# One transpose moved ahead of another, small VectorE operands placed in PSUM, one more pair of h scaled on VectorE, and new queue orders on four engines

## What is computed

```python
# conv: a decaying, turning filter along the 1024 positions, from a first state
y = (ifft(fft(filt) * fft(xn)) + last_conv * phazor_progression * phazor) * gate   # its real part
# ffn: every operand is first quantised in blocks of 16 along its last axis
scale = max(max(abs(block)) / 6, 1e-12)
q = nearest_of(0, .5, 1, 1.5, 2, 3, 4, 6)(abs(block / scale)) * sign * scale
h = silu(q(xn) @ q(w_gate).T) * (q(xn) @ q(w_up).T)                                # 352 wide
ffn = q(h) @ q(w_down).T
```

## Time and profile before

| | us |
|---|---|
| median of 3 runs | 121.84 (121.81 to 121.91) |
| the profiled execution | 121.87, span 119.9 |
| TensorE busy | 112.0 |
| VectorE busy | 102.8 |
| ScalarE busy | 100.9 |
| GpSimd busy | 99.7 |

### The profile page before, as it was taken

How to read it: one execution, slowest core, us unless ns; L and a number is a source line. 1 busy time by engine, 2 the same in 40 slices (tenths; PEclk the granted TensorE clock), 3 DMA queues, 4 the chain that set the end, 5 groups by cost and what they waited for, 6 DMA issues and landing times.

```text
span 119.9 us, 2356 instructions
## 1 busy us (share of the span) xinstructions
PE 112.0 (93%) x665; PEld 82.2 (69%) x666; DVE 102.8 (86%) x218; ACT 100.9 (84%) x221; POOL 99.7 (83%) x125
## 2 busy tenths in 40 slices
PE   6999798767999999999999999999999999999992
PEld 2643555234668687767797878688777977989791
DVE  0899999999499999999997999799969999999400
ACT  5759999699997999996899989978997759688950
POOL 4662087989999999999999999999899999999200
PEclk9999999999999999999999999999999999999999
DMA  3992000000000000020002000200002002011112
GB/s 111 322 353 106 3 0 0 3 3 0 5 0 0 0 0 5 0 87 0 0 0 96 0 0 3 87 0 0 5 0 87 0 0 87 5 46 41 53 59 66
DMA packets 3324, 4.90 MB, mean 41 GB/s; under 512 B 497, under 2 KB 1393, under 8 KB 3313
## 3 DMA queue, kind: packets, MB, share of 16 engines
q1 hardware_dynamic: 3168, 4.77, 11.3%
q10 hardware_dynamic: 144, 0.00, 0.1%
HBM read 2.67 MB, written 2.10 MB: 40 GB/s over the span
## 4 chain that ended last, share of the span: by engine, by line
PE 73%; POOL 8%; ACT 6%; DVE 4%; DMA 3%; issue 2%; SPq 1%; POOLq 0%; DVEq 0%; ACTq 0%
PE ps_o L1324 17%; PE ps_g L1248 15%; PE ps_u L1263 14%; PE ps_h L1282 9%; PE ps_u L1270 6%; DMA w_raw<-w_in 3%; PE ps_x L1208 3%; PE ps_o L1310 3%; PE ps_x L1231 3%; POOL vec L468 2%; PE ps_o L1313 2%; DVE ps_u L1632 1%; ACT xbig L840 1%; ACT xsq L833 1%; ACT xq_T L854 1%
## 5 line engine op out<-in xcount | busy, mean ns | idle before, releaser
L1248 PE MATMUL ps_g<-wg_T,xq_T 128*128 128x352 f32 x64 | 24.8, 468 | 1.2 <-ACT xq_T L854 0.7
L1324 PEld LDWEIGHTS ps_o<-wd_T,hq_T 128*128 128x128 f32 x174 | 21.6, 192 | 2.3 <-issue 1.0
L1324 PE MATMUL ps_o<-wd_T,hq_T 128*128 128x128 f32 x174 | 23.1, 276 | 0.0
L1263 PE MATMUL ps_u<-wu_T,xq_T 128*128 128x352 f32 x64 | 22.2, 464 | 0.0
L867 ACT COPY hq_T<-ps_h 128x384 f32<-128x384 f32 x32 | 15.3, 478 | 5.0 <-PE ps_h L1282 4.9
L1686 DVE TENSOR_TENSOR ps_u<-silu,ps_u 128x704 f32<-128x704 f32 (+1 forms) x17 | 14.3, 844 | 2.2 <-PE ps_u L1263 2.1
L861 ACT ACTIVATE silu<-ps_g 128x352 f32<-128x352 f32 x32 | 14.8, 464 | 1.6 <-PE ps_g L1248 1.5
L1282 PE MATMUL ps_h<-ident,hq 128*128 128x128 f32 x96 | 15.9, 274 | 0.3 <-ACT hq_T L867 0.2
L1282 PEld LDWEIGHTS ps_h<-ident,hq 128*128 128x128 f32 x96 | 11.7, 142 | 5.6 <-issue 4.1
L1768 DVE TENSOR_TENSOR ps_u<-ps_u,inv 128x704 f32<-128x704 f32 (+1 forms) x17 | 14.4, 850 | 0.3
L1692 DVE TENSOR_REDUCE ps_u<-ps_u 128x44 f32<-128x704 f32 (+1 forms) x17 | 14.4, 852 | 0.2
(11 more groups left out here) (182 smaller groups left out, 252.2 us busy)
## 6 DMA issues: line engine op xcount, KB each, us to landing
x_all<-x_in SPq DMA_DIRECT2D x8, 256.0 KB, 4.7
out<-x_all SPq DMA_DIRECT2D x7, 256.0 KB, 2.0
w_raw<-w_in SPq DMA_DIRECT2D x2, 192.0 KB, 3.8
out<-x_all SPq DMA_DIRECT2D x4, 64.0 KB, 1.5
w_raw<-w_in SPq DMA_DIRECT2D x1, 176.0 KB, 3.9
par<-params_in ACTq DMA_DIRECT2D x1, 3.5 KB, 2.9
```

The source lines that it names most:

```text
L1248: pe.matmul(ps_g[:, 0:I], x_cols(t), wg_T[:, :], start=True, stop=True).then_inc(s_gate, 1)
L1263: pe.matmul(slot(q)[:, j, 0:I], x_cols(t), wu_T[:, :], start=True, stop=True).then_inc(s_up, 1)
L1324: m = pe.matmul(out_cols(t), hq_T[t % NHT][:, c * P:(c + 1) * P], wd_T[:, c, :], start=False, stop=(c == NCH - 1), skip_group_check=True)
```

## The change

Five things change. First, TensorE turns xn of group 0 ahead of the quantised x of group 1 (`XN_FIRST`); both use ps_x. Second, small VectorE operands move from SBUF to PSUM: the block maxima of the weights and of x of groups 0 to 2, the inverses of the two first weights and of x of group 0, and half of rstd. The inverses of w_down stay in SBUF and get a step and a semaphore of their own (`down_inverses`). Third, pair 4 leaves `BY_POOL`, so VectorE scales it, and `copy_codes(4)` and `scale_codes(4)` fall away. Fourth, groups 0, 2, 3 and 5 are normalised on ScalarE in place of 0 to 3, so group 1 goes to GpSimd and group 5 to ScalarE. Fifth, the call orders of all four engines are new, with one filler fewer. `late_step` is new too, but isn't called (`STAT_POOL` is False).

```diff
-    XN_ACT = (0, 1, 2, 3)
-    BY_POOL = (4, 6, 8, 10)
+    XN_ACT = (0, 2, 3, 5)
+    BY_POOL = (6, 8, 10)
+    STAT_POOL = False
+    XN_FIRST = True
...
+        def weight_inverse(n):
+            return slot(1)[:, n, NCH * P:NCH * P + NCH * P // BLK]
+        def weight_row(n):
+            a = NCH * P + NCH * P // BLK
+            return slot(1)[:, n, a:a + (NCH * P // BLK, WB - NCH * P // BLK)[n]]
+        half_rs = slot(0)[:, 1, 508:508 + TG]
+        def first_row(n, k):
+            a = (XBG // 2) * k
+            return ps_o[:, a:a + XBG // 2] if n else ps_x[:, GT // 2 + a:GT // 2 + a + XBG // 2]
+        def x_row(g):
+            return slot(g - 1)[:, 1, I:I + XBG]
+        def wait_x_bank(eng, g):
+            if g == 1:
+                eng.wait_ge(*((s_xnTc, 1) if XN_FIRST else (s_xqTc, 1)))
+            elif g == 2 and XN_FIRST:
+                eng.wait_ge(s_xqTc, x_done(1))
+            elif g >= 2:
+                eng.wait_ge(s_xnTc, g - 1)
...
             def divide_down():
-                pool.wait_ge(s_winv, 2)
+                pool.wait_ge(s_dinv, 1)
...
             def turn_xn(g):
                 wait_xn(pe, g)
-                if g < NG - 1:
+                if g == 0 and XN_FIRST:
+                    pe.wait_ge(s_xqTc, 1)
+                elif g < NG - 1:
                     pe.wait_ge(s_xqTc, x_done(g + 1))
...
             def weight_maxima(n):
...
+                dve.wait_ge(s_open0, 1)
-                dve.tensor_reduce(w_amax[:, W_BLKS[n]], blocks(w_raw[:, cols]), X_AXIS, ALU.max,
+                dve.tensor_reduce(weight_row(n), blocks(w_raw[:, cols]), X_AXIS, ALU.max,
...
+            def down_inverses():
+                dve.wait_ge(s_wden, 2)
+                dve.reciprocal(w_inv[:, :], w_den[:, GU // BLK:]).then_inc(s_dinv, 1)
```

More of the change, by code:

```diff
@@ L114, in build @@
         shift = sb("shift", [P, NT])
+        late = sb("late", [P, 3, NT])
         xc = sb("xc", [P, GT])
@@ L1130, in _ @@
             open_last(29)
+            square_h(16)
+            copy_hT(29)
+            big_h(16)
             open_last(30)
             open_last(31)
-            copy_hT(29)
             copy_hT(30)
@@ L1344, in _ @@
             gate_tile(1)
-            up_tile(1)
-            up_tile(2)
             up_tile(3)
+            in_table(0)
+            turn_xn(0)
             gate_tile(2)
-            turn_weight(2)
             gate_tile(3)
-            in_table(0)
             in_table(1)
+            turn_xq(1, 1)
             round_h(0)
-            turn_xq(1, 1)
             gate_tile(4)
+            turn_h(0)
             up_tile(4)
-            turn_xn(0)
-            round_h(1)
             gate_tile(5)
@@ L1360, in _ @@
             up_tile(5)
-            up_tile(6)
-            up_tile(7)
-            turn_h(0)
-            gate_tile(6)
             turn_h(1)
             sum_down(0)
+            gate_tile(6)
+            round_h(1)
+            sum_down(1)
+            up_tile(6)
             turn_h(2)
-            sum_down(1)
             gate_tile(7)
+            up_tile(7)
+            turn_xq(2, 1)
+            sum_down(2)
             turn_h(3)
-            turn_xq(2, 1)
-            round_h(2)
             gate_tile(8)
@@ L1384, in _ @@
-            round_h(3)
             turn_xq(3, 1)
-            gate_tile(11)
-            sum_parts(1)
             up_tile(10)
             up_tile(11)
+            turn_h(6)
             gate_tile(12)
-            turn_h(6)
-            sum_parts(2)
-            sum_parts(3)
+            sum_down(4)
+            sum_down(5)
+            gate_tile(13)
+            turn_xn(2)
             round_h(4)
-            turn_xn(2)
-            gate_tile(13)
+            turn_h(7)
+            sum_down(6)
@@ L1397, in _ @@
+            gate_tile(14)
             up_tile(12)
             up_tile(13)
-            sum_down(4)
-            turn_h(7)
-            gate_tile(14)
-            sum_down(5)
-            sum_down(6)
-            round_h(5)
+            turn_xq(4, 1)
             gate_tile(15)
             turn_h(8)
-            turn_xq(4, 1)
+            round_h(5)
+            gate_tile(16)
+            turn_xn(3)
+            turn_h(9)
+            gate_tile(17)
             up_tile(14)
-            turn_h(9)
@@ L1424, in _ @@
             sum_down(8)
             sum_down(9)
+            sum_down(10)
             round_h(7)
+            turn_h(13)
             turn_xq(5, 1)
-            gate_tile(19)
-            turn_h(11)
-            sum_down(10)
+            sum_down(11)
             up_tile(18)
             up_tile(19)
+            turn_h(14)
             gate_tile(20)
             turn_xn(4)
-            turn_h(12)
             sum_parts(8)
+            sum_parts(9)
+            round_h(8)
+            sum_parts(10)
@@ L1437, in _ @@
+            sum_parts(11)
             gate_tile(21)
-            sum_parts(9)
-            sum_parts(10)
-            sum_down(11)
-            sum_parts(11)
-            round_h(8)
-            turn_h(13)
-            gate_tile(22)
-            sum_down(12)
             up_tile(20)
             up_tile(21)
-            turn_h(14)
+            gate_tile(22)
+            turn_h(15)
+            turn_xq(6, 1)
+            gate_tile(23)
+            sum_down(12)
             sum_down(13)
-            turn_xq(6, 1)
+            sum_down(14)
@@ L1451, in _ @@
+            turn_h(16)
             round_h(9)
-            gate_tile(23)
-            turn_h(15)
+            gate_tile(24)
             turn_xn(5)
+            sum_down(15)
+            turn_h(17)
             up_tile(22)
             up_tile(23)
-            turn_h(16)
-            sum_down(14)
-            sum_down(15)
-            gate_tile(24)
-            turn_h(17)
-            round_h(10)
-            gate_tile(25)
             sum_parts(12)
             sum_parts(13)
-            up_tile(24)
@@ L1467, in _ @@
-            up_tile(25)
-            gate_tile(26)
-            turn_h(18)
             sum_parts(14)
             sum_parts(15)
+            gate_tile(25)
+            turn_h(18)
+            round_h(10)
+            gate_tile(26)
+            sum_down(16)
+            up_tile(24)
+            sum_down(17)
+            up_tile(25)
+            turn_h(19)
+            sum_parts(16)
+            sum_down(18)
             round_h(11)
+            sum_parts(17)
+            sum_parts(18)
+            sum_parts(19)
```

630 lines of the change are left out of this document (335 added, 295 removed).

## The result

The changed kernel takes 121.3 us (median of 21 runs, 120.61 to 121.74), the kernel before 121.92 in the 21 runs beside it (121.66 to 122.45). The ratio is 0.9945, with a 95% interval of 0.9933 to 0.9958: 0.67 us faster. The forecast was 1.4 us, so its sign was right and its size double the measured one.

The account below looks back on a forecast made before the run. TensorE, busy 112.0 of 119.9 us, was taken as the fullest engine, its time movable only through start, waits and end. 1.33 plus 0.3 minus 0.2 gave 1.4 us: 121.84 - 1.4 = 120.4 us, range 119.3 to 121.8.

Parts of the forecast that it names:

- lead at gate_tile(8), with the 0.07: TensorE at gate_tile(8): starts at 38.37 instead of 39.63 us, plus 0.07 for different work ahead; lead 1.33 us.
- from there to up_tile(31): TensorE's list behind 39 us: may win 0.3 us by having no waits to 54 us.
- from up_tile(31) to sum_down(31): Matmuls of the end: a tighter end loses 0.2 us, with waits of 0.4 or somewhat more.
- from sum_down(31) to the end: Last copy and store: they stay as they are, 2.3 us.
- The waits behind it: TensorE, 27 to 39 us: turn_h(0) waits 0.3, round_h(1) 0.5 for big_h(1), sum_down(1) 0.7 us for copy_hT(1).
- GpSimd's six steps: Polynomial steps in GpSimd's opening: 0.36 us each assumed start to start; before, 0.26 each but one 0.79.
- VectorE's extra 0.80: Scaling pair 4 on VectorE: 0.80 us more by start-to-start, hidden by some 2.8 us of idle in the middle.
- A: VectorE becomes the limit and the lead is eaten: 121.7 us, no change; chance 0.14.
- B: GpSimd's set-up chain no faster than now, holding ScalarE at square_x(1) and TensorE behind silu(2): 123.0 us; chance 0.10.
- the last pair's chain: End, on VectorE, ScalarE and TensorE: needs about 8.9 us, against some 9.5 us of matmuls behind up_tile(31).
- The bounds are 0 and 0.34: VectorE's opening: divide_weight(1) with inverses in PSUM takes 0.55 instead of 0.89 us, a gain of 0.34.
- rival C: Small operands do not take the contention away, divide_weight(1) stays at 0.89, opening 0.35 later: 120.7 us; chance 0.12.

Follow-up runs that it names:

- store_apart: Changed kernel with only copy_last(29) put ahead of copy_hT(31) on ScalarE; 121.07 us, ratio 0.9934 to the kernel before.
- down_late: Changed kernel with the quantising of w_down late again, divide_down behind part_turns on GpSimd and ScalarE's steps moved to match; 126.67 us, ratio 1.0387 to the kernel before.
- again2: The changed kernel itself, unaltered, measured once more beside the kernel before; 121.09 us, ratio 0.9929.

## Why the forecast was right in sign and double in size

Its terms, and what the two traces give:

```
term                                           forecast   measured
lead at gate_tile(8), with the 0.07              +1.33      +1.72   (39.63 - 37.98 + 0.07)
from there to up_tile(31)                        +0.3       -0.17   (1.55 left there)
from up_tile(31) to sum_down(31)                 -0.2       -0.52   (9.91 became 10.43)
from sum_down(31) to the end                      0         -0.36   (3.17 became 3.53)
sum                                              +1.4       +0.67
```

*The opening held, step by step.* divide_weight(1) 0.55 as worked out; divide_x(1) at 19.40 for 19.7; gate_tile(4) at 27.12 for 27.60; the one long wait of TensorE stands before gate_tile(3) and is put down to a silu. It is 1.33 us by the stations where I had 1.75. These 0.42 us are what the opening earned beyond the forecast (0.39 at gate_tile(8)). The waits behind it came out as forecast: 0.41, 0.48 and 0.67 for 0.3, 0.5 and 0.7. One station missed: the list was to start at 15.10 and starts at 15.27, but what gate_tile(3) waits for doesn't hang on that. GpSimd's six steps took 0.26 each, none 0.79.

*Pair 4 held.* From 40 to 105 us TensorE is busy 65.00 of 65.00 us (64.92 before), so VectorE's extra 0.80 is covered, and the two reversals show that what the edit brings is ScalarE's copy and GpSimd's scaling. Rivals A and B did not come about; B's mechanism exists and was priced too low.

*What failed are the terms behind gate_tile(8), the end above all.* Together they fell 1.15 us short, and it was luck that 0.39 more from the opening hid a third of that. For the end I wrote "minus 0.2 for a tighter end" and "The last copy and store stay". I had set the last pair's chain (8.9) against TensorE's matmuls (9.5) and found it just covered, with "waits of 0.4 or somewhat more". I did not follow ScalarE's list there: copy_out(6) ahead of copy_hT(28), with one round less of TensorE between the two turns. TensorE waits 0.74 there, and the way from up_tile(31) to sum_down(31) grows by 0.52. The next 0.36 is the store issue, which no row of before shows and which I took as fixed. The largest single miss is the middle, -0.17 where I had +0.3. That term was a hope from a list followed only to 54 us, and the present small waits, 0.93 in all, did not go but became 1.11, in steps of under 0.2 us each; without it and with 0.52 for 0.2, the sum is 0.8 (1.33 - 0.52), close to what came.

*One price was wrong in a way that didn't show in the sum.* "The bounds are 0 and 0.34" for the small operands came from the neighbour that the division has now. The change itself brings a longer neighbour. The measured gain of that one edit in the old order is 0.5 to 0.7, since GpSimd's chain also moves. In the new order the operands' place is worth 2.8 us, and rival C, had it come true, would have cost about that and not 0.35: the new order needs the operands in PSUM.

## What to carry to other kernels

Price a hold-up between two engines by the instruction that will stand beside it after the change, not by the one there now. A lead won in the opening reaches the end only as far as every other engine's list is moved with it: follow all lists, ScalarE's copies and GpSimd's long steps too, through the last pair, before any gain of the opening goes into the sum. When one wait has been moved, look in the new trace for what released the next one: the two reversals of pair 4 cost the same time through two different engines. And undo each part alone in both orders; here the placement of the operands, without any reordering, gave 0.5 to 0.7 of the 0.7 to 0.9 us.

## What the runs showed of the hardware that was not expected

*The start follows the arrival of the weights.* In all 18 profiles VectorE's reduction of the later weights starts 0.07 to 0.17 us behind the landing of their transfer. In 12 of the 13 profiles with the new opening and its operands in PSUM, the first matmul of the list starts 8.70 to 8.73 us behind VectorE's reduction of the later weights, and that reduction starts between 6.15 and 7.39. In the 13th, store_apart, it is 9.20, but gate_tile(4) comes 20.51 us behind the reduction, as in the others (20.50 to 20.56, without down_late), which is why its waits to gate_tile(8) are the smallest of the table. In the changed kernel VectorE is idle ahead of that reduction (0.32 at 6.56, row shown with the result); in the kernel before it starts at 6.56 with no idle shown. again2, with the reduction at 6.24, has the span of 118.51. It may be why runs of the changed kernel spread over 1.1 us and those of before over 0.8; the timed runs have no trace, so this is not shown.

*A store's issue has no fixed price.* 332 ns in every kernel with the old end, 0.57 to 1.12 us for one of four with the new one, at the same place each time. What decides the length stays open.
